# First self attention of a two-layer perceiver: projections moved ahead of the mix on TensorE, with ScalarE's copies in the same order

## The chip, the cores and the metric

One core of one Trainium2 chip runs the whole program. The metric is the device time of one execution in microseconds, the median of several. The kernel before takes 2668.17 us (median of 3, from 2666.99 to 2670.02).

## What is computed

Six stages work on a residual `x` of 64 sequences of 32 tokens with 256 features, which is 2048 rows. The change touches the code of the self attention, which is used twice, and alters the order in its first use only, the second of the six stages:

```
x = x + cross_attention_0(ctx, layernorm(x))
x = x + self_attention_0(layernorm(x))          # this stage
x = x + mixture_of_experts(layernorm(x))
x = x + cross_attention_1(layernorm(x), ctx)
x = x + self_attention_1(layernorm(x))          # rotary, through a latent
x = x + tanh_map(layernorm(x))

def self_attention_0(x):                        # 16 heads of 16 features
    q, k, v = x @ Wq.T, x @ Wk.T, x @ Wv.T      # by head
    q, k = rms_norm(q, qn_w), rms_norm(k, kn_w)
    attn = softmax(q @ k.T / 4)                 # 32 x 32 in each sequence and head
    return (attn @ v, heads side by side) @ Wo.T
```

## The kernel before, in words

The residual lies in SBUF as 16 tiles of 128 rows, so a tile holds 4 sequences. `self_attention` (line 1970) writes the code of each engine as one function `step(n, has)`, which `steps` calls for n from -6 to 16. `has(i)` says whether tile n+i exists. There is no scheduler: each engine goes through its own list in the order written, and semaphores tie the lists together. In one step the engines work on tiles of different age.

TensorE (`step` at the end of the function) does in step n:

- `scores(n+1)`: 64 products of 32x32 (L2317) into columns 0 to 127 of banks 4 to 7. It waits until the queries and keys of its tile are copied, and, by `past(pe, s.yT, n - 1)`, until the mix of the tile two before it has been copied out of the same banks.
- `queries_keys_T(n+2)`: 8 transposes (L2293) into banks 2 and 3.
- `rows_T(n+5)`: 2 transposes of the normalised rows (L2252) into bank 0.
- `output(n-1)`: 2 products (L2341) into the lower half of bank 1.
- `mix(n)`: 64 products of 32x32 (L2331), probabilities by values, into columns 128 to 191 of banks 4 to 7. It waits for the transposed probabilities and for `s.shift` of tile n+1, which says that VectorE has read the scores out.
- `values(n+4)` (2 products of 256 columns) and `project(n+4)` (2 products of 512 columns, queries and keys side by side), both at L2259. `project` writes bank 2, and so waits for the copies of queries and keys of tile n+2 out of banks 2 and 3.

A float32 product appears in the trace as two matmuls, each with a weight load of its own, and a transpose as one. So `scores` and `mix` are 128 matmuls and 128 weight loads each.

ScalarE does in step n: `queries_T(n+2)` (L2196), `exps(n+1)` (L2215), `keys_T(n+2)` (L2202), `rows_T(n+5)` (L2159), `mix_T(n)` (L2221, the copy `yT`), `values(n+4)` (two copies, L2186), `inner(n+4)` (squares, L2173, and the raw copy, L2175). VectorE does the softmax of tile n+1, adds the output of tile n-1 to the residual and takes its statistics, then rows, `queries_keys(n+3)` (L2058) and `key_sums(n+4)` (L2032). GpSimd turns those sums into inverse roots (L119, L122).

The same function, with `rotary` true, is the second self attention. Its order has one more product and larger projections.

Of the kernel before, what the change touches and what calls it, by code (L numbers as in the profile page):

```python
# [1813 lines left out]
class PlainWeights:  # L1814

    rotary = False
# [19 lines left out]
class RotaryWeights:  # L1836

    rotary = True
# [131 lines left out]
def self_attention(kit, stage, weights, norm, ahead, extra, after):  # L1970
# [4 lines left out]
    rotary, wm = weights.rotary, weights.m  # L1975
# [6 lines left out]
    with kit.stage() as st:  # L1982
# [23 lines left out]
        def past(engine, sem, value):  # L2006

            if value > 0:
                engine.wait_ge(sem, value)
# [6 lines left out]
        with nc.Block(no_gpsimd_drain=True) as block:  # L2016
# [136 lines left out]
            @block.scalar  # L2153
            def _(act):
                def rows_T(n):
                    act.wait_ge(s.xlT_ps, n + 1)

                    past(act, s.qk_ps, (n - 1) * (2 if rotary else 1))
                    nc.scalar.copy(m.xlT[:, n % 2].rearrange("p f t -> p (f t)"), kit.psum(0)[:, 0:D]).then_inc(s.xlT, 1)  # L2159

                def inner(n):
                    if rotary:

                        past(act, s.turned, n * 2)
                        for i in range(2):
                            act.wait_ge(s.qk_ps, n * 2 + i + 1)
                            if i == 1:
                                act.wait_ge(s.cosed, n * 2 + 1)
                            nc.scalar.copy(r.lat[:, i * H:(i + 1) * H, :], kit.psum(2 + i).rearrange("p (h l) -> p h l", h=H)).then_inc(s.lat, 1)
                    else:  # L2170
                        act.wait_ge(s.qk_ps, n + 1)
                        past(act, s.ss, n)
                        nc.scalar.activation(r.sq[:], kit.psum(2), ACT.Square).then_inc(s.sq, 1)  # L2173
                        past(act, s.qk, n - 1)
                        nc.scalar.copy(r.raw[:, n % 2], kit.psum(2)).then_inc(s.raw, 1)  # L2175

                def values(n):
                    act.wait_ge(s.v_ps, n + 1)
                    if n == 0:
                        act.wait_ge(s.zero, n_zero)  # L2180

                    past(act, s.y_ps, n - VB + 1)
                    src = kit.psum(1)[:, D:2 * D].rearrange("p (a i e) -> p a i e", i=2, e=EV)
                    dst = m.v[:, n % VB].rearrange("p (a i) l -> p a i l", i=2)
                    for i in range(2):
                        nc.scalar.copy(dst[:, :, i, i * EV:(i + 1) * EV], src[:, :, i, :]).then_inc(s.v, 1)  # L2186

                def queries_T(n):
                    act.wait_ge(s.qT_ps, n + 1)
                    if rotary:  # L2190
                        past(act, s.qrT_ps, n)
                        nc.scalar.copy(r.qrT[:], kit.psum(2)).then_inc(s.qrT, 1)
                    else:
                        act.wait_ge(s.gain, 1)
                        past(act, s.s_ps, n - 1)
                        nc.scalar.activation(m.qT[:, n % 2].rearrange("p c t -> p (c t)"), kit.psum(2), ACT.Identity, scale=r.gain[:]).then_inc(s.qT, 1)  # L2196

                def keys_T(n):
                    act.wait_ge(s.kT_ps, n + 1)

                    past(act, s.s_ps, n - 1)
                    nc.scalar.copy(m.kT[:, n % 2].rearrange("p c t -> p (c t)"), kit.psum(3)).then_inc(s.kT, 1)  # L2202

                def latent_T(n):
                    act.wait_ge(s.qrT_ps, n + 1)
                    if n == 0:
                        act.wait_ge(s.qb, 1)
                    past(act, s.s_ps, n - 1)
                    nc.scalar.activation(m.qT[:, n % 2].rearrange("p c t -> p (c t)"), kit.psum(2), ACT.Identity, bias=r.qb[:], scale=LS).then_inc(s.qT, 1)

                def exps(n):
                    act.wait_ge(s.shift, n + 1)

                    past(act, s.pT, n)
                    nc.scalar.activation(m.prob[:].rearrange("p h k -> p (h k)"), m.score[:].rearrange("p h k -> p (h k)"), ACT.Exp).then_inc(s.p, 1)  # L2215

                def mix_T(n):
                    act.wait_ge(s.y_ps, n + 1)

                    past(act, s.o_ps, n)  # L2220
                    nc.scalar.copy(m.yT[:].rearrange("p f (b q) -> p b f q", b=BT), mixed).then_inc(s.yT, 1)  # L2221

                def step(n, has):
                    if has(2):
                        queries_T(n + 2)
                    if has(1):
                        exps(n + 1)
                    if has(2):
                        keys_T(n + 2)
                    if has(5):  # L2230
                        rows_T(n + 5)
                    if has(0):
                        mix_T(n)
                    if rotary and has(2):
                        latent_T(n + 2)
                    if has(4):
                        values(n + 4)
                        inner(n + 4)
                    if extra is not None and n == -4:
                        extra.first_copy(act)  # L2240
                    if extra is not None and n == -3:
                        extra.second_copy(act)

                steps(step)

            @block.tensor
            def _(pe):
# [52 lines left out]
                def scores(n):  # L2300
                    if n == 0 and extra is not None:

                        pe.wait_ge(extra.w, 1)
                    pe.wait_ge(s.qT, n + 1)
                    pe.wait_ge(s.kT, n + 1)

                    past(pe, s.yT, n - 1)
                    if rotary:
                        if n == 0:
                            pe.wait_ge(s.masked, 1)  # L2310
                        for a in range(BT):
                            nc.tensor.matmul(kit.all[:, 4 + a, 0:P], kit.ident16[:], r.causal[:].rearrange("p c k -> p (c k)"), start=True, stop=False, skip_group_check=True)
                    for c in range(HC):
                        for b in range(BT):
                            for a in range(BT):
                                rows, tokens = slice(a * S, (a + 1) * S), slice(b * S, (b + 1) * S)
                                mm = nc.tensor.matmul(score[tokens, a, c, :], m.qT[rows, n % 2, c, tokens], m.kT[rows, n % 2, c, tokens],  # L2317
                                                      start=not rotary, stop=True, skip_group_check=True)
                    mm.then_inc(s.s_ps, 1)

                def mix(n, more):
                    pe.wait_ge(s.pT, n + 1)

                    if more:
                        pe.wait_ge(s.shift, n + 2)
                    for f in range(FC):
                        for i in range(2):
                            for a in range(BT):
                                for b in range(BT):
                                    rows, part, h = slice(b * S, (b + 1) * S), slice(a * S, (a + 1) * S), f * 2 * BT + 2 * a + i  # L2330
                                    mm = nc.tensor.matmul(mixed[part, b, f, :], m.v[rows, n % VB, h, :], m.pT[rows, n % 2, place(h), :],  # L2331
                                                          start=(i == 0), stop=(i == 1), skip_group_check=True)
                    mm.then_inc(s.y_ps, 1)
# [10 lines left out]
                def step(n, has):  # L2344
                    if has(1):
                        scores(n + 1)
                    if has(2):
                        queries_keys_T(n + 2, has(3))
                    if has(5):
                        rows_T(n + 5)  # L2350
                    if has(-1):
                        output(n - 1)
                    if has(0):
                        mix(n, has(1))
                    if rotary and has(2):
                        latent_T(n + 2)
                    if has(4):
                        values(n + 4)
                        project(n + 4)

                    if extra is not None and n == -4:
                        extra.first_product(pe)
                    if extra is not None and n == -3:
                        extra.second_product(pe)
# [756 lines left out]
```

## Time and profile before

| | before |
|---|---|
| median of the runs | 2668.17 us (3 runs, 2666.99 to 2670.02) |
| profiled execution, its own time | 2681.12 us |
| span of its trace | 2679.3 us |
| busy in the span | TensorE 91%, VectorE 64%, GpSimd 55%, ScalarE 48% |
| mean granted TensorE clock | 0.965 of full |
| first self attention, first transpose to last matmul | 1279.9 to 1447.9 us of the span |

The span is cut in the page into 40 slices of 67 us, so this stage is a little more than the 20th and 21st. Shares of the whole span say little about it. It is read from the timeline of its engines, window by window. A row of the timeline merges equal instructions that follow each other: start, length, engine, line, names, shape and count, and in square brackets the idle time of that engine just before them with what ended it. "issue" there is time in which the engine waited for nothing that the profile shows.

### The profile page before, as it was taken

The page shows a single profiled execution, that of the slowest core. Times are in us where ns is not written, and L with a number is a line of the kernel's source. Part 1 is how long each engine was busy: PE and PEld are TensorE (multiplying, and loading weights), DVE is VectorE, ACT ScalarE, POOL GpSimd, SP SyncE. Part 2 cuts the span into 40 slices and gives each one's busy share as a digit, 9 for nine tenths or more (in the row PEclk, how much of TensorE's full clock was granted, in tenths as well). Part 3 has the DMA queues.
Part 4 walks back from the last instruction along what each step waited for, and adds up shares of the span by engine and source line. Part 5 has one row for each costly group of instructions (what it writes and reads, how often), then busy time and mean ns, then how long its engine had stood idle before and what let it go on. Part 6 is the DMA issues. An engine that isn't in the chain of part 4 may idle for free. (4 is left out here: it accounts for less than half of the span.)

```text
span 2679.3 us, 64293 instructions
## 1 busy us (share of the span) xinstructions
PE 2450.1 (91%) x24481; PEld 1903.1 (71%) x24481; DVE 1704.3 (64%) x3966; ACT 1279.7 (48%) x2969; POOL 1469.7 (55%) x1670
## 2 busy tenths in 40 slices
PE   5887999999999999998797989489999999998997
PEld 2445887788788878786465578368888888886665
DVE  5666868687878786774475833366566665653665
ACT  2454656565656565654342323144454445443443
POOL 5776767575757576754672245555456446322333
PEclk9999999999999999998897999699999999999998
DMA  4233121111112111210003359532334234210001
GB/s 149 110 119 98 41 54 49 35 44 39 46 33 49 39 43 36 49 27 12 29 5 107 124 164 286 160 121 78 84 95 98 71 69 105 61 52 14 3 4 34
DMA packets 223075, 190.04 MB, mean 71 GB/s; under 512 B 88705, under 2 KB 210514, under 8 KB 222770
## 3 DMA queue, kind: packets, MB, share of 16 engines
q1 hardware_dynamic: 206386, 151.19, 18.8%
q0 software_dynamic: 10080, 30.00, 4.6%
q10 hardware_dynamic: 6304, 4.72, 0.6%
q8 instruction: 198, 3.24, 0.5%
q14 instruction: 107, 0.88, 0.1%
HBM read 151.53 MB, written 34.31 MB: 69 GB/s over the span
## 5 line engine op out<-in xcount | busy, mean ns | idle before, releaser
L288 POOL TENSOR_TENSOR rk<-ss,neg_half 128x32 f32<-128x32 f32 x64 | 348.7, 5448 | 246.8 <-DVE ss L270 246.8
L1695 PE MATMUL banks<-rowsT,qk 128*128 128x257 f32 x1024 | 243.3, 380 | 0.8 <-ACT qk L1622 0.8
L321 ACT ACTIVATE ksq<-kT 128x512 f32<-128x512 f32 x256 | 161.6, 631 | 160.7 <-DVE kT L264 160.5
L264 DVE COPY kT<-banks 128x512 f32<-128x512 f32 x256 | 177.0, 692 | 61.4 <-PE banks L375 56.8
L375 PE MATMUL banks<-x_hi,wk_hi 128*128 128x256 f32 x1024 | 213.1, 289 | 1.0 <-DVE kT L264 1.0
L1695 PEld LDWEIGHTS banks<-rowsT,qk 128*128 128x128 f32 x1024 | 189.5, 190 | 27.6 <-ACT qk L1622 1.2
L375 PE MATMUL banks<-x_hi,wk_lo 128*128 128x256 f32 x1024 | 206.3, 284 | 0.0
L375 PE MATMUL banks<-x_lo,wk_hi 128*128 128x256 f32 x1024 | 205.2, 281 | 0.5 <-DVE x_lo L256 0.5
L1172 ACT ACTIVATE score<-score,ntop 128x289 f32<-128x289 f32 x256 | 135.9, 533 | 118.3 <-DVE ntop L1055 118.3
L1543 POOL CAST r_hi<-diff 128x512 fp32r<-128x512 f32 x64 | 42.5, 664 | 259.5 <-PE banks L1721 256.9
L1516 POOL DMA_INDIRECT parts<-scratch_expert,address x128 | 132.0, 1031 | 92.4 <-DVE residual L1414 45.8
L375 PEld LDWEIGHTS banks<-x_hi,wk_hi 128*128 128x128 f32 x1024 | 159.1, 189 | 3.5 <-issue 3.0
L375 PEld LDWEIGHTS banks<-x_lo,wk_hi 128*128 128x128 f32 x1024 | 159.7, 190 | 0.8 <-DVE x_lo L256 0.7
L375 PEld LDWEIGHTS banks<-x_hi,wk_lo 128*128 128x128 f32 x1024 | 158.1, 188 | 0.0
L1603 ACT ACTIVATE prob<-banks,ntop 128x257 f32<-128x257 f32 x256 | 120.3, 479 | 70.1 <-DVE ntop L1430 66.9
L1430 DVE TENSOR_REDUCE ntop<-banks 128x2 f32<-128x514 f32 x128 | 88.6, 692 | 99.9 <-PE banks L1695 99.9
L1052 DVE CUSTOM_DVE_ANT_0 score<-banks,rkb 128x289 f32<-128x289 f32 x256 | 107.9, 457 | 66.0 <-PE banks L1239 57.9
L1611 ACT CAST p_hi<-banks 128x512 fp32r<-128x512 f32 x128 | 68.8, 589 | 162.6 <-PE banks L1704 153.6
L2259 PE MATMUL banks<-w,xlT 128*128 128x512 f32 (+1 forms) x320 | 133.3, 550 | 1.1 <-ACT kT L2202 0.9
L1186 ACT COPY mix<-banks 128x512 f32<-128x512 f32 x128 | 75.1, 587 | 112.1 <-PE banks L1265 112.1
L1721 PE MATMUL banks<-p_hi,r_hi 128*128 128x512 f32 x256 | 112.5, 439 | 4.3 <-ACT p_hi L1611 4.3
L1443 DVE TENSOR_TENSOR p_lo<-banks,p_hi 128x512 fp32r<-128x512 f32 x128 | 82.4, 686 | 51.3 <-ACT p_hi L1611 50.6
(369 smaller groups left out, 6544.1 us busy)
## 6 DMA issues: line engine op xcount, KB each, us to landing
rowsT<-in_ctxT SPq DMA_DIRECT2D x64, 257.0 KB
wgu<-in_expert_gu SPq DMA_DIRECT2D x64, 256.0 KB
rows<-in_ctx SPq DMA_DIRECT2D x64, 256.0 KB
raw<-in_ctx SPq DMA_DIRECT2D x61, 256.0 KB
scratch_qT<-qT SPq DMA_DIRECT2D x16, 512.0 KB, 2.6
scratch_kT<-kT SPq DMA_DIRECT2D x16, 512.0 KB, 3.0
q<-scratch_qT SPq DMA_DIRECT2D x64, 128.0 KB
kT<-scratch_kT SPq DMA_DIRECT2D x64, 128.0 KB
```

The lines of the kernel that those rows point to most:

```text
L264: nc.vector.tensor_copy(m.kT[:, k, 2 * i:2 * i + 2, 0:ROWS], banks[i % 2].rearrange("p (a r) -> p a r", a=2)).then_inc(s.kT, 1)
L288: nc.gpsimd.tensor_tensor(m.rk[:], m.ss[:], kit.neg_half[:, 0:KF * H], ALU.pow).then_inc(s.rk, 1)
L321: nc.scalar.activation(m.ksq[:, 2 * i:2 * i + 2, :], m.kT[:, k, 2 * i:2 * i + 2, 0:ROWS], ACT.Square).then_inc(s.ksq, 1)
L375: mm = nc.tensor.matmul(banks[i % 2][:, a * ROWS:(a + 1) * ROWS], w[:, f, pr * P:(pr + 1) * P], x[:, k, f, :], start=(at == 0), stop=(at = ...
L1052: nc.vector.tensor_tensor_reduce(m.score[:, c, :], score[c][:, 0:NK], m.rkb[:, c, :], 1.0, -3.0e38, ALU.mult, ALU.max, m.top[:, c:c + 1]). ...
L1172: nc.scalar.activation(m.score[:, c, :], m.score[:, c, :], ACT.Exp, bias=m.ntop[:, c:c + 1], accum_out=m.mass[:, c:c + 1]).then_inc(s.p, 1)
L1430: nc.vector.tensor_reduce(m.ntop[:, n % 2, h * HALF:(h + 1) * HALF], score[h][:, :, 0:CTX], AX.X, ALU.max, negate=True).then_inc(s.ntop, 1)
L1516: nc.gpsimd.indirect_dma_start(m.parts[:, t % 2, c, :], None, d.expert_rows, bass.IndirectOffsetOnAxis(kept.address[:, t, c:c + 1], 0)).th ...
L1603: nc.scalar.activation(m.prob[:, k, c, :], score[h][:, c - h * HALF, 0:CTX], ACT.Exp, bias=m.ntop[:, k, c:c + 1], accum_out=m.mass[:, k, c ...
L1695: mm = nc.tensor.matmul(score[h][:, c - h * HALF, 0:CTX], m.qk[:, f, j, c * BT:(c + 1) * BT, :].rearrange("p h q -> p (h q)"), m.rowsT[:, ...
L1721: mm = nc.tensor.matmul(kit.bank[3][:, f, :], lhsT, rhs, start=(at == 0), stop=(at == len(terms) - 1))
L2259: mm = nc.tensor.matmul(out, m.xlT[:, n % 2, f, :], w[:, f, columns], start=(f == 0 and not rotary), stop=(f == FC - 1))
```

## The change

For the first self attention (`rotary` false) TensorE's step ends with `project(n+4)`, `values(n+4)`, `mix(n)` in place of `mix(n)`, `values(n+4)`, `project(n+4)`. ScalarE copies the keys before it takes the exponentials, and does `inner(n+4)`, `values(n+4)`, `mix_T(n)` in place of `mix_T(n)`, `values(n+4)`, `inner(n+4)`. In both self attentions `scores` has one wait more, `past(pe, s.shift, n)`. No arithmetic changes.

```diff
@@ ScalarE
                         queries_T(n + 2)
-                    if has(1):
+                    if rotary and has(1):
                         exps(n + 1)
                     if has(2):
                         keys_T(n + 2)
+                    if not rotary and has(1):
+                        exps(n + 1)
                     if has(5):
                         rows_T(n + 5)
-                    if has(0):
-                        mix_T(n)
-                    if rotary and has(2):
-                        latent_T(n + 2)
-                    if has(4):
-                        values(n + 4)
-                        inner(n + 4)
+                    if rotary:
...
+                    else:
+
+                        if has(4):
+                            inner(n + 4)
+                            values(n + 4)
+                        if has(0):
+                            mix_T(n)
@@ TensorE, scores
                     pe.wait_ge(s.kT, n + 1)
 
+                    past(pe, s.shift, n)
                     past(pe, s.yT, n - 1)
@@ TensorE, step
-                    if has(0):
-                        mix(n, has(1))
-                    if rotary and has(2):
-                        latent_T(n + 2)
-                    if has(4):
-                        values(n + 4)
-                        project(n + 4)
+                    if rotary:
...
+                    else:
+
+                        if has(4):
+                            project(n + 4)
+                            values(n + 4)
+                        if has(0):
+                            mix(n, has(1))
```

In the middle of the stage, TensorE's list is this before (each row `x64` is one `scores` or one `mix`):

```order
L2317 MATMUL banks<-kT,qT 32x32 x64
L2293 MATMUL banks<-ident,qk 128x128 x8
L2252 MATMUL banks<-ident,xl 128x128 x2
L2341 MATMUL banks<-wo,yT 128x256 x2
L2331 MATMUL banks<-pT,v 32x32 x64
L2259 MATMUL banks<-w,xlT 128x256 x2
L2259 MATMUL banks<-w,xlT 128x512 x2
L2317 MATMUL banks<-kT,qT 32x32 x64
```

and this in the changed kernel, whose lines are numbered some ten higher:

```order
L2328 MATMUL banks<-kT,qT 32x32 x64
L2303 MATMUL banks<-ident,qk 128x128 x8
L2262 MATMUL banks<-ident,xl 128x128 x2
L2352 MATMUL banks<-wo,yT 128x256 x2
L2269 MATMUL banks<-w,xlT 128x512 x2
L2269 MATMUL banks<-w,xlT 128x256 x2
L2342 MATMUL banks<-pT,v 32x32 x64
L2328 MATMUL banks<-kT,qT 32x32 x64
```

The two projections now stand between the output and the mix, and nothing stands any more between a mix and the next scores.

ScalarE's list in one step of the same place, before:

```order
L2196 ACTIVATE qT<-banks,gain 128x512
L2215 ACTIVATE prob<-score 128x512
L2202 COPY kT<-banks 128x512
L2159 COPY xlT<-banks 128x256
L2221 COPY yT<-banks 128x4x2x32
L2186 COPY v<-banks 128x8x16 x2
L2173 ACTIVATE sq<-banks 128x512
L2175 COPY raw<-banks 128x512
```

and in the changed kernel:

```order
L2196 ACTIVATE qT<-banks,gain 128x512
L2202 COPY kT<-banks 128x512
L2215 ACTIVATE prob<-score 128x512
L2159 COPY xlT<-banks 128x256
L2173 ACTIVATE sq<-banks 128x512
L2175 COPY raw<-banks 128x512
L2186 COPY v<-banks 128x8x16 x2
L2221 COPY yT<-banks 128x4x2x32
```

The copy of the keys is one place earlier, and the copy `yT` of the mix, for which the next scores wait, is last.

## Rows read from the trace of the kernel before

**Rows 1.** The page: span, and the granted TensorE clock in 40 slices.

```profile
span 2679.3 us, 64293 instructions
...
PEclk9999999999999999998897999699999999999998
```

**Rows 2.** Timeline of TensorE (PE), one step of the stage, scores to scores.

```profile
1346.00 1.29 PE L2317 MATMUL banks<-kT,qT 32*32 32x32 f32 x128
1347.33 1.06 PE L2293 MATMUL banks<-ident,qk 128*128 128x128 f32 x8
...
1348.44 1.03 PE L2341 MATMUL banks<-wo,yT 128*128 128x256 f32 x4
1349.40 1.31 PE L2331 MATMUL banks<-pT,v 32*32 32x32 f32 x128
1350.64 2.85 PE L2259 MATMUL banks<-w,xlT 128*128 128x256 f32 x8
1353.42 0.34 PE L2317 MATMUL banks<-kT,qT 32*32 32x32 f32 x32
```

**Rows 3.** Timeline of ScalarE (ACT), the same step.

```profile
1349.37 0.57 ACT L2202 COPY kT<-banks 128x512 f32<-128x512 f32 x1
...
1350.76 0.37 ACT L2221 COPY yT<-banks 128x256 f32<-128x256 f32 x1 [0.54 <-PE banks L2331]
```

**Rows 4.** Timeline of VectorE (DVE) and GpSimd (POOL), the same step.

```profile
1346.80 0.68 DVE L2032 TENSOR_REDUCE ss<-sq 128x32 f32<-128x512 f32 x1
...
1347.87 5.43 POOL L122 TENSOR_TENSOR rss<-rss,neg_half 128x32 f32<-128x32 f32 x1
...
1349.51 0.42 DVE L2086 TENSOR_TENSOR residual<-residual,banks 128x256 f32<-128x256 f32 x1 [0.71 <-PE banks L2341]
...
1350.95 0.68 DVE L2072 TENSOR_REDUCE mass<-prob 128x16 f32<-128x512 f32 x1
...
1353.60 0.69 DVE L2058 TENSOR_TENSOR qk<-raw,rss 128x512 f32<-128x512 f32 x1
```

**Rows 5.** Windows: twelve steps; then two at half clock (TensorE alone).

```profile
1307.71:1416.38 108.67, 96.11 (x3332) 67.69 (x3331) 74.71 (x152) 47.09 (x107) 73.89 (x33) 0.94 0.02 4
...
1324.10:1327.40 3.30, 3.30 (x5) 0.50 0.03 5
...
1412.80:1416.10 3.30, 3.30 (x6) 0.50 0.02 5
```

**Rows 6.** Waits of TensorE in those twelve steps: total us, times, longest.

```profile
PE banks L2331 <- issue: 9.1, 5, 2.2
PE banks L2341 <- issue: 1.5, 3, 0.7
PE banks L2293 <- DVE qk L2058: 0.8, 1, 0.8
PE banks L2331 <- DVE score L2067: 0.7, 1, 0.7
```

**Rows 7.** Timeline of TensorE around a mix that stops halfway.

```profile
1367.67 0.25 PE L2331 MATMUL banks<-pT,v 32*32 32x32 f32 x5 [1.27 <-issue]
...
1374.19 1.02 PE L2331 MATMUL banks<-pT,v 32*32 32x32 f32 x97
1377.39 0.35 PE L2331 MATMUL banks<-pT,v 32*32 32x32 f32 x31 [2.17 <-issue]
1377.67 4.54 PE L2259 MATMUL banks<-w,xlT 128*128 128x256 f32 x8
```

**Rows 8.** Timeline of TensorE, last steps: no projections are left there.

```profile
1420.99 0.34 PE L2331 MATMUL banks<-pT,v 32*32 32x32 f32 x28 [0.38 <-issue]
1422.00 1.04 PE L2317 MATMUL banks<-kT,qT 32*32 32x32 f32 x100 [0.66 <-ACT yT L2221]
1425.34 0.34 PE L2317 MATMUL banks<-kT,qT 32*32 32x32 f32 x28 [2.30 <-issue]
```

**Rows 9.** DMA queue of one engine's instructions from 1301 to 1446 us.

```profile
q8 instruction: 35, 0.57, 1.6%
```

**Rows 10.** Windows of TensorE's matmuls (first) and weight loads (second), same stretch.

```profile
1301.00:1446.00 145.00, 121.35 (x4407) 0.90 0.02 4
...
1301.00:1446.00 145.00, 86.56 (x4405) 0.90 0.02 4
```

More of the change, by code:

```diff
@@ L2229, in step @@
                         keys_T(n + 2)
+                    if not rotary and has(1):
+                        exps(n + 1)
                     if has(5):
                         rows_T(n + 5)
-                    if has(0):
-                        mix_T(n)
-                    if rotary and has(2):
-                        latent_T(n + 2)
-                    if has(4):
-                        values(n + 4)
-                        inner(n + 4)
+                    if rotary:
+                        if has(0):
+                            mix_T(n)
+                        if has(2):
+                            latent_T(n + 2)
+                        if has(4):
[3 more added lines that the diff above has]
+                        if has(4):
+                            inner(n + 4)
+                            values(n + 4)
+                        if has(0):
+                            mix_T(n)
                     if extra is not None and n == -4:
@@ L2352, in step @@
                         output(n - 1)
-                    if has(0):
-                        mix(n, has(1))
-                    if rotary and has(2):
-                        latent_T(n + 2)
-                    if has(4):
-                        values(n + 4)
-                        project(n + 4)
+                    if rotary:
+                        if has(0):
+                            mix(n, has(1))
+                        if has(2):
+                            latent_T(n + 2)
+                        if has(4):
+                            values(n + 4)
+                            project(n + 4)
+                    else:
+                        if has(4):
+                            project(n + 4)
+                            values(n + 4)
+                        if has(0):
+                            mix(n, has(1))
                     if extra is not None and n == -4:
```

## The prediction

> **What bounds the kernel now.** I read the page first [rows 1]: 2679.3 us of span, 2.4 us under the execution's own 2681.12, and a clock row that dips in the slices of this stage. The page is an average over six stages, so I went to the timeline of the first self attention. In an undisturbed step TensorE goes from one scores to the next in 1353.42 - 1346.00 = 7.42 us, and its pieces follow each other without a gap worth the name [rows 2]: scores from 1346.00, transposes, output, mix from 1349.40, projections from 1350.64. TensorE itself is the bound. The nearest rival for it is the loop over GpSimd: sums at 1346.80, a root of 5.43 us, `qk` at 1353.60 [rows 4]. With its hand-offs this loop needs about 7.2 us, so no step can fall much under that, and the most that an unblocked loop could give is 0.2 us a step.
>
> Most steps are not undisturbed. From scores(1) to scores(13) there are twelve, and they take 108.67 us [rows 5], 19.6 more than 12 x 7.42 = 89.0. Two things fill these 19.6 us. First, TensorE stands idle 9.1 + 1.5 + 0.8 + 0.7 = 12.1 us [rows 6], 9.1 of it in the middle of mixes, for no releaser that the profile shows ("issue"). Second, four stretches of 3.4 us run at half clock, 1.2 GHz, of which the first and last stand in [rows 5]. The projections inside take 4.54 us [rows 7] in place of 2.85 [rows 2], 1.69 more each time, 6.8 us in all. Together that is 18.9 of the 19.6.
>
> **What the stops are.** Count the instructions between the two stops of [rows 7], at 1367.67 and 1377.39: 5 matmuls of mix, 8 of projections, 128 of scores, 8 and 2 transposes, 4 of output, 97 of mix make 252, with as many weight loads 504, and with the eight bare waits of a step 512, twice 256. Over the stage there are 4407 matmuls and 4405 loads [rows 10], with some 120 waits about 8930, and the instruction queue moved 35 packets of 16 KB [rows 9]: one for each 255. So TensorE's instructions come in blocks of 256, and the stops are at block ends: the next block has not arrived. In the undisturbed step a block lasts 256/564 x 7.42 = 3.4 us and nothing stops. The block that a 32x32 burst (256 instructions in 1.25 us) eats quickly is the one that comes late.
>
> The Trainium skill says otherwise in "Runtime: NRT & Kernel Launch", section "Instruction fetch mechanics": the sequencer fetches the next 16 KiB block (256 instructions) by itself, and crossing a boundary is mostly hidden, since instructions issue more slowly than blocks arrive. The block size agrees with the trace; the hiding does not, with 2.17 us of stop at one boundary. If no stop were left, the sum below would be 7.8 - 19.6 = -11.8 us, and this is the second rival.
>
> **What the change does, step by step.** No instruction is taken away; 28 bare waits are added, 14 in each self attention, on a value that an earlier wait has already seen. I price them at nothing: they stand where TensorE waits anyway or is issue-bound, and the rows of the trace put no busy time on such waits. They do move the block ends in all later stages. The second self attention is the only one with 32x32 bursts; its stops could shift by 2 us either way.
>
> Projections before mix: `project` now waits for the copy of the keys, 1349.37 + 0.57 = 1349.94 before [rows 3], while the output ends at 1349.47 [rows 2]. Because the keys' copy changes places with the exponentials, it ends about 0.6 us earlier, 1349.3, and the wait is covered. With the old order on ScalarE it would have been 0.5 us a step. The exponentials come 0.4 us later; the sum that reads them starts at 1350.95 [rows 4], over 1 us after they end, so nothing follows. `values` needs the addition of tile n-1, which ends at 1349.93 [rows 4] and has the 1.9 us of `project` as cover. The squares start 2 us earlier; the GpSimd loop takes at most 0.2 us a step from that, and TensorE, the bound, takes nothing. Mix no longer meets the wait for `shift`: 0.7 us once [rows 6].
>
> **Term 1, the copy of the mix.** Before, the 2.85 us of projections hid the copy `yT`. Now scores(n+2) stands right behind mix(n) and waits for it. The price is in the stage's last steps, where no projections are left and the order is already the new one: scores sits idle 0.66 us for `yT` [rows 8]. The copy alone is 0.37 us [rows 3]. So 0.4 to 0.7; I take 0.65, the row for the same wait. 12 x 0.65 = 7.8 us.
>
> **Term 2, instruction blocks.** Mix and scores are now 512 instructions in 1.25 + 0.65 + 1.29 us. Two block ends always fall in it, 256 instructions apart, hence 1.9 us apart, and a block needs longer. The same place in the last steps shows it: the block that begins at 1420.99 ends at 1425.34, 4.35 us, with 2.30 us of stop in the middle of scores [rows 8]. On the other side, 3.4 us a block runs unhindered [rows 2], so a block that can be asked for at once costs at most 3.4 - 1.9 = 1.5. I expect 1.4 where the boundary falls early in the mix, and 2.3 where it falls so late that the sequencer must first get past the `yT` wait; a third of the steps are of the second kind, mean 1.75. 12 x 1.75 = 21 us (ends: 0 and 12 x 2.4 = 29). The stops in the middle of mixes go: the mix now follows 4.9 us of slow instructions.
>
> **Term 3, clock.** Before, the clock fell to 1.2 GHz behind the stop of 2.17 us and not behind that of 1.27 [rows 7]. The changed step has 0.65 + 1.4 to 2.3 us idle inside 4.5 to 5.5 us of nothing but small matmuls, and what follows is slow at half clock. I take six of twelve steps, 6 x 1.69 = 10.1 us (ends: 0 and 20.3).
>
> Sum: 89.0 + 7.8 + 21 + 10.1 = 127.9 us for the twelve steps in place of 108.67, **+19.3 us**. Before the first mix and after the last projection the order hardly differs. From the profiled 2681.12 this gives 2700.4; the runs shown have a median 13 us lower, and from 2668.17 it gives **2687.5**.
>
> **Rivals.**
> 1. Only the copy costs: stops and clock stay as frequent as before, merely at other places. +7.8, 2676.0. For it: the number of blocks is the same. Against: [rows 8], where each adjacent pair stops. 12%.
> 2. Faster: the stops of mixes go with the half-clock stretches behind them, and scores stops no longer than for `yT`, because the block is fetched meanwhile. 7.8 - 19.6 = -11.8, 2656.4. It decides below 19.6/12 = 1.6 us added a step. The skill's rule would give this. For it: blocks of 3.4 us never stopped. Against: 1.9 us is far below 3.4. 10%.
> 3. The worst of terms 2 and 3 at once: 2.4 us of stop in each step and half clock in each. 7.8 + 29 + 20.3 - 19.6 = +37.5, 2705.7. For it: the block of 4.35 us. 11%.
> 4. No difference: a half-hidden copy and short stops that balance what goes. The pieces moved have slack on all other engines, so this needs a coincidence. 2668. 5%.
>
> **How the numbers follow.** My forecast has 62%; its own range is 2677 (no half clock, +9.2) to 2698 (half clock always, +29.5). The range for 8 in 10 leaves out rival 2, the upper part of rival 3 and most of rival 4: 2671 to 2704. A measurement of this kernel tells 0.2%, 5.3 us, from no change. Faster by more: rival 2, 10%. Within: rival 4 and a little of rival 1, 6%. Slower by more: 84%.
>
> **What would show it.** In the trace after: an idle of about 0.65 us before scores, ended by `yT`, in all twelve steps; stops by "issue" of 1.4 to 2.4 us inside scores, once a step, and none in mixes; steps of about 9.8 us at full clock and 11.5 with half clock; no wait of `project` for `kT`. Stops left in mixes and none in scores would make term 2 wrong; a clock that stays at 1.00 through the stage, term 3; steps of 8.1 us, rival 1 or 2.

## The result, and the profile after

The changed kernel takes 2689.72 us (median of 4, 2687.74 to 2692.46), the kernel before 2667.58 (4 runs, 2664.18 to 2670.02): ratio 1.0085, 95% interval 1.0067 to 1.0102. That is 22.1 us slower, where 19.3 were forecast.

First the page of the changed kernel: its span, and the granted clock in 40 slices, beside [rows 1].

```profile
span 2685.9 us, 64321 instructions
...
PEclk9999999999999999998887999799999999999998
```

The span is only 6.6 us longer than in [rows 1], not 22. Two windows explain most of it, each read in both kernels: the stage of this change, and the stage of the experts two stages later. Columns are the stretch, its length in us, busy us and count for TensorE, weight loads, VectorE, ScalarE, GpSimd, then clock, DMA share and GB/s. Before:

```profile
1559.80:1682.10 122.30, 105.88 (x767) 95.65 (x767) 43.46 (x128) 38.05 (x128) 60.80 (x64) 0.97 0.82 256
1276.80:1445.90 169.10, 136.05 (x4445) 95.55 (x4445) 103.84 (x205) 63.28 (x144) 107.15 (x55) 0.86 0.04 14
```

After, the same two in the other order:

```profile
1276.70:1470.40 193.70, 147.50 (x4444) 110.21 (x4445) 104.03 (x205) 61.80 (x144) 105.43 (x55) 0.79 0.04 12
...
1585.60:1692.80 107.20, 101.90 (x766) 94.75 (x766) 43.32 (x128) 41.58 (x128) 60.64 (x64) 0.95 0.89 292
```

The changed stage is 24.6 us longer. The experts' stage, which the change does not touch, was 15.1 us shorter. The two GB/s figures are no cause of this: 256 x 122.3 and 292 x 107.2 are the same bytes. In the profiled execution of the kernel before TensorE waited there for VectorE's `hidT`:

```profile
PE banks L3024 <- DVE hidT L2959: 11.5, 17, 1.3
```

A later trace of the same kernel has 0.3 us of this wait, and 106.6 us for the whole stage (run `before_again` below). Why the first trace waited is not shown. So the comparison of two single spans says 6.6 us because of an accident in another stage; the changed stage says 24.6 and the runs say 22.1.

Now the twelve steps from scores(1) to scores(13), beside the first line of [rows 5], and TensorE's waits in them, beside [rows 6]:

```profile
1307.22:1439.76 132.54, 105.22 (x3332) 80.94 (x3332) 75.68 (x154) 46.47 (x110) 72.09 (x35) 0.83 0.02 4
```

```profile
PE banks L2328 <- issue: 13.9, 8, 2.8
PE banks L2328 <- ACT yT L2221: 6.3, 11, 0.6
PE banks L2303 <- issue: 1.9, 1, 1.9
PE banks L2262 <- issue: 1.5, 1, 1.5
PE banks L2352 <- issue: 1.4, 1, 1.4
PE banks L2342 <- issue: 1.0, 2, 0.6
PE banks L2269 <- ACT kT L2202: 0.8, 1, 0.8
```

They take 132.5 us in place of 108.7. L2328 is scores, L2342 the mix, L2303 and L2262 transposes, L2352 the output, L2269 the projections. The stops of mixes, 9.1 us before, are 1.0; the scores now stop, 13.9 us in eight steps, and wait 6.3 us for `yT`, which they never did in these steps before. With the mean clock at 0.83, 2 x 0.17 x 132.5 = 45 us of the twelve steps ran at half clock, against 2 x 0.06 x 108.7 = 13 before.

One step of the timeline of TensorE, beside [rows 2]:

```profile
1349.30 0.71 PE L2328 MATMUL banks<-kT,qT 32*32 32x32 f32 x61 [0.56 <-ACT yT L2221]
1351.41 0.91 PE L2328 MATMUL banks<-kT,qT 32*32 32x32 f32 x67 [1.41 <-issue]
1352.25 1.97 PE L2303 MATMUL banks<-ident,qk 128*128 128x128 f32 x8
...
1355.44 2.74 PE L2269 MATMUL banks<-w,xlT 128*128 128x512 f32 x8
1358.12 1.29 PE L2342 MATMUL banks<-pT,v 32*32 32x32 f32 x128
1359.96 0.46 PE L2328 MATMUL banks<-kT,qT 32*32 32x32 f32 x35 [0.56 <-ACT yT L2221]
1361.82 0.91 PE L2328 MATMUL banks<-kT,qT 32*32 32x32 f32 x68 [1.40 <-issue]
```

Scores waits for the copy of the mix, does 61 of its 128 matmuls, stands 1.41 us for nothing the profile can name, and goes on. (The last row is cut off by the window; that scores has 128 too.) The transposes behind it take 1.97 us in place of 1.06 [rows 2]: half clock. From one scores to the next it is 10.7 us in place of 7.42. In the next step the stop comes behind matmul 35 and not 61. That is 26 matmuls, with their loads 52 instructions, earlier, and 52 is what the 564 instructions of a step have over 512, twice 256.

### The profile page after: what moved, and what is told of

Read it like the earlier page. It is cut to its first block and busy times, and to the rows that moved or that the text cites. A ratio compares the mean times of both kernels' runs of the same rounds, so it can differ in the third digit from the quotient of the medians.

```text
span 2685.9 us, 64321 instructions
## 1 busy us (share of the span) xinstructions
PE 2457.7 (92%) x24481; PEld 1918.1 (71%) x24481; DVE 1702.9 (63%) x3966; ACT 1280.3 (48%) x2969; POOL 1465.3 (55%) x1670
## 5 line engine op out<-in xcount | busy, mean ns | idle before, releaser
L2269 PE MATMUL banks<-w,xlT 128*128 128x512 f32 (+1 forms) x320 | 128.6, 535 | 2.0 <-ACT kT L2202 2.0
```

The lines of the kernel that those rows point to most:

```text
L2269: mm = nc.tensor.matmul(out, m.xlT[:, n % 2, f, :], w[:, f, columns], start=(f == 0 and not rotary), stop=(f == FC - 1))
```

## The experiments

Theory A, the forecast's: with the projections moved away, mix and scores are 512 instructions in one piece; the next block of 256 is late, TensorE stops, and half clock follows. Theory B: only the new wait for `yT` and what hangs on it costs, 0.65 us a step or 7.8 in all; by its size alone it does not reach 22 us. The kernel before itself took 2667.6 to 2689.4 us on the chips used, so each whole time is compared with the kernel before on its own chip, and the two orders with each other only within one group of runs. "Twelve steps" is read in each trace from scores(1) to scores(13).

**`again`**: the changed kernel, unedited.

> The changed kernel once more, beside the runs below, so that they have it on the same chip. Both theories: about 22 us above the kernel before.

Measured: ratio 1.0069 (1.0050 to 1.0088), 2706.09 against 2687.68 us, 18.4 more. Twelve steps 129.5 us. On a second chip the change costs about the same, 18.4 us for 22.1.

**`dense`**: the changed kernel with work added between mix and scores.

```diff
+                def filler(n):
+                    pe.wait_ge(s.xlT, min(n + 2, NT))
+                    for f in range(2 * FC):
+                        nc.tensor.matmul(kit.psum(0)[:, D:2 * D], m.xlT[:, n % 2, f % FC, :], w[:, f % FC, 0:D], start=True, stop=True)
...
                         if has(0):
                             mix(n, has(1))
+                        if has(0) and has(4):
+                            filler(n + 4)
```

> The changed kernel with four products of 256 columns more (8 matmuls, 1.7 us at full clock) between each of the first twelve mixes and the scores behind it. Theory A (what the change costs is that 512 instructions of 32x32 products stand in one piece: their blocks come late, TensorE idles and then runs at half clock): the added work covers the wait for yT (0.6 us) and most of the wait for the block (1.4 to 1.8 us), and the clock stays up, so the twelve steps take 118 to 126 us, less than the 132.5 of the changed kernel although work was added; the whole is 6 to 15 us faster than the changed kernel. Theory B (the change costs only the wait for yT and the slower chain behind it): 1.7 - 0.6 = 1.1 us more a step, 13 us slower than the changed kernel.

Measured, on the chip of `again`: ratio 1.0044 (1.0025 to 1.0062), 2699.92 us, 6.2 us faster than the changed kernel, with products added that take 1.9 us from their start to the next scores, 23 us in twelve steps. The twelve steps as a window, and TensorE's waits in them:

```profile
1308.90:1433.50 124.60, 113.59 (x3427) 84.11 (x3426) 75.66 (x154) 45.52 (x110) 72.51 (x35) 0.99 0.02 4
```

```profile
PE banks L2333 <- issue: 7.3, 8, 1.9
PE banks L2347 <- issue: 1.6, 4, 0.6
```

No wait for `yT` is left, the stops in scores (L2333) fall from 13.1 us in `again` to 7.3, and the clock rises from 0.86 to 0.99. Adding useless work made the twelve steps 4.9 us shorter than in `again`. Theory B wanted 13 us more; it is out as the whole cause. The added products change three things at once, the wait, the stops and the clock, so `dense` does not say which of them gave how much.

**`split_p`**: TensorE does project, mix, values; ScalarE squares and raw copy, `yT`, values.

```diff
                         if has(4):
                             project(n + 4)
-                            values(n + 4)
                         if has(0):
                             mix(n, has(1))
+                        if has(4):
+                            values(n + 4)
```

> Order project, mix, values (ScalarE: squares and raw copy, yT, values). The 0.9 us of values stand between mix and scores and cover the wait for yT. Theory A: two block ends are now 2.2 us apart in place of 1.9, so a stop of about 1.2 us stays in most scores; twelve steps 109 to 118 us, the whole 3 to 12 us slower than the kernel before. Theory B (only the wait for yT costs): no wait is left, so as fast as the kernel before within 3 us.

Measured: ratio 0.9995 (0.9977 to 1.0013): no difference from the kernel before. The twelve steps, and the largest of TensorE's waits in them:

```profile
1309.50:1425.60 116.10, 96.20 (x3331) 68.76 (x3330) 75.60 (x153) 46.26 (x108) 72.61 (x34) 0.96 0.02 4
```

```profile
PE banks L2329 <- issue: 11.9, 9, 2.2
PE banks L2343 <- issue: 2.8, 4, 0.8
PE banks L2263 <- issue: 1.7, 1, 1.7
PE banks L2304 <- issue: 1.6, 1, 1.6
```

L2329 is scores, L2343 the mix. With the smaller ones there are 19.1 us of stops, as many as in the changed kernel (19.7). What has gone is the wait for `yT` and most of the half clock: 2 x 0.04 x 116.1 = 9 us in place of 45. That the twelve steps are 7.4 us longer than in [rows 5] is within theory A's range, but its forecast for the whole kernel, 3 to 12 us slower, missed: it was 1.7 us faster, and the interval leaves at most 3.5 us of cost (0.13%). Theory B's forecast for the whole was met. So this run does not decide between the two. It does show that 0.9 us of work between mix and scores removes the cost of the change within the error of the runs, though the stops stay.

**`keys_late`**: the changed kernel, exponentials ahead of the keys' copy on ScalarE.

> The changed kernel with ScalarE's exponentials ahead of the keys' copy, as before. Both theories: project waits for kT about 0.5 us in each step, behind the output. Theory A: the blocks still bind, so the twelve steps are 3 to 8 us longer than in the changed kernel. If the wait for kT was covered by something else: no difference.

Measured: ratio 1.0072 (1.0049 to 1.0094), 1.4 us above the changed kernel. Twelve steps 130.3 us against 129.5, where 3 to 8 more were expected. A miss: `project` waits for `kT` once, 0.7 us. In the step from 1361.47 the transposes run at half clock, as TensorE's timeline shows:

```profile
1364.27 1.97 PE L2301 MATMUL banks<-ident,qk 128*128 128x128 f32 x8
1366.03 0.51 PE L2260 MATMUL banks<-ident,xl 128*128 128x128 f32 x2
1366.38 1.03 PE L2350 MATMUL banks<-wo,yT 128*128 128x256 f32 x4
1367.36 2.82 PE L2267 MATMUL banks<-w,xlT 128*128 128x512 f32 x8
```

and on ScalarE's timeline of the same step:

```profile
1366.53 0.58 ACT L2202 COPY kT<-banks 128x512 f32<-128x512 f32 x1
```

The keys' copy ends at 1367.11, late as feared, but output ends only at 1367.41. The slow clock behind the stop hides what would show at full clock. The one step with the wait agrees: there the transposes behind the stop and the output run at full clock, and the output's 1.03 us end before the copy does.

```profile
1432.91 0.70 PE L2301 MATMUL banks<-ident,qk 128*128 128x128 f32 x5 [1.84 <-issue]
1433.45 1.03 PE L2350 MATMUL banks<-wo,yT 128*128 128x256 f32 x4
1435.15 2.82 PE L2267 MATMUL banks<-w,xlT 128*128 128x512 f32 x8 [0.67 <-ACT kT L2202]
```

So that part of the change neither costs nor gains here that the runs could tell.

**`b16`** and **`a16`**: the kernel before and the changed kernel with queries and keys of this stage stored as bfloat16. A product of `scores` is then one matmul and one load, not two.

```diff
-... qT=([P, 2, HC, P], F32), kT=([P, 2, HC, P], F32), ...
+... qT=([P, 2, HC, P], F32 if rotary else BF16), kT=([P, 2, HC, P], F32 if rotary else BF16), ...
```

> The kernel before with the copies of queries and keys of the first self attention stored as bfloat16, so that each of the 64 products of scores is one matmul and one load in place of two; scores are computed from rounded queries and keys. A step has 436 TensorE instructions in place of 564. Theory A: blocks last 4.3 us, most stops in mixes go and the half clock with them: twelve steps 88 to 97 us in place of 108.7, the whole 10 to 20 us faster than the kernel before. If stops have nothing to do with instructions: only 0.6 us a step of scores go, 7 us at most.

> The changed kernel with the same bfloat16 copies. Mix and scores are together 384 instructions, so in about half of the steps only one block ends in them. Theory A: stops in half of the steps, twelve steps 97 to 110 us in place of 132.5; the gap between the two orders shrinks from 22 us to 4 to 13. Theory B (only the wait for yT): the gap stays what it was, since the wait is the same.

Measured, on one chip: `b16` 0.9910 (0.9890 to 0.9929), 24.7 us faster than the kernel before; `a16` 0.9936 (0.9915 to 0.9957), 16.3 us faster. The gap between the orders is 8.4 us in the runs (18.4 and 22.1 at full width), 15.3 in the twelve steps (23.9 at full width). The first window is `b16`, the second `a16`:

```profile
1307.50:1399.80 92.30, 80.12 (x2570) 57.83 (x2570) 73.86 (x151) 47.09 (x107) 74.22 (x33) 1.00 0.02 4
```

```profile
1306.50:1414.10 107.60, 89.95 (x2563) 66.28 (x2562) 75.13 (x154) 45.97 (x110) 72.73 (x33) 0.90 0.01 3
```

In `b16` the stops in mixes shrink from 9.1 to 2.7 us and the clock stays at 1.00, so a halved scores is worth 16.4 us in the twelve steps, of which its own shorter run explains 12 x 0.65 = 8. TensorE is no longer alone in binding there: it waits 7.4 us in eleven steps for ScalarE's copy `raw`. In `a16` the wait for `yT` is still 6.3 us, exactly that of the full-width change, while stops are 4.4 + 3.4 us and the clock is 0.90. In the runs the gap has shrunk by more than half, as theory A forecast (4 to 13 us), and not stayed, as B's forecast had it. But 8.4 us is no more than the 7.8 of the wait alone, so it is the trace, with 15.3 us, more stops and the lower clock, that speaks against B.

**`phase_b`** and **`phase_a`**: 64 bare waits more at the start of TensorE's list, in the kernel before and in the changed one.

```diff
                 pe.wait_ge(weights.loaded, weights.count)
+                if not rotary:
+                    for _ in range(128):
+                        pe.wait_ge(weights.loaded, weights.count)
```

The built list holds two of these waits in one instruction: the trace of `phase_b` has 64 semaphore instructions for the added line.

> The kernel before with 64 bare waits more at the start of TensorE's list of the first self attention, on a semaphore that is already there. Nothing else moves. Theory A: every block end stands 64 instructions earlier in the work, so each stop is found at another place of a mix or scores, by exactly 64 instructions; the time changes by less than 5 us, either way. If stops are tied to the work and not to the count of instructions: they stay where they were.

> The changed kernel with the same 64 waits. Theory A: the stops in scores move by 64 instructions and stay, one in each step; the time is within 5 us of the changed kernel.

Measured: `phase_b` 0.9983 (0.9969 to 0.9997), 4.5 us faster; `phase_a` 1.0085 (1.0058 to 1.0111), twelve steps 136.3 us. mix(1) in the kernel before, then in `phase_b`:

```profile
1319.60 1.25 PE L2331 MATMUL banks<-pT,v 32*32 32x32 f32 x125
1322.81 0.25 PE L2331 MATMUL banks<-pT,v 32*32 32x32 f32 x3 [1.96 <-issue]
```

```profile
1328.15 0.99 PE L2331 MATMUL banks<-pT,v 32*32 32x32 f32 x93
1331.33 0.46 PE L2331 MATMUL banks<-pT,v 32*32 32x32 f32 x35 [2.19 <-issue]
```

The stop has moved by 32 matmuls, which with their loads are 64 instructions. The edit leaves the work of the mix as it was; what moved is the count of instructions ahead of it. So the stops are tied to that count, and the ends of instruction blocks are what fits it. In `phase_a` the same holds for scores: the changed kernel stops behind matmul 114, 88 and 61 of scores(3), (4) and (5), and `phase_a` behind 82, 56 and 29, each 32 fewer. Ten stops in scores take 18.7 us: another phase, about the same cost.

**`act_only`**: ScalarE's new order with TensorE's old one.

> ScalarE's new order with TensorE's old one. Both theories agree that TensorE's order has to be followed: the copy yT stands behind the squares, the raw copy and the copies of values, and these wait for the projections behind the mix, so scores(n+2) waits for them, 1.9 us a step (0.60 + 0.58 + 0.43 + 0.37 less overlap). Theory A adds that this pause lies between the projections and scores, so it gives the instruction blocks time: stops in mixes get shorter. Twelve steps 120 to 132 us, the whole 12 to 22 us slower than the kernel before.

Measured: 1.0096 (1.0061 to 1.0131), 25.9 us slower; twelve steps 141.0 us, more than forecast.

```profile
PE banks L2328 <- ACT yT L2221: 20.6, 11, 1.9
PE banks L2328 <- issue: 7.1, 3, 2.9
PE banks L2342 <- issue: 4.6, 4, 1.9
```

The forecasts, 120 to 132 us and 12 to 22 us slower, both missed. The wait for `yT` is 1.9 us a step as worked out. The stops in mixes did get shorter, 4.6 us in place of 9.1, but 7.1 us appeared in scores, and with those of transposes and output all stops are 15.9 us in place of 10.6. The clock is 0.88, which is 2 x 0.12 x 141.0 = 34 us at half clock, though no mix stands next to a scores here. So ScalarE's new order with TensorE's old one costs about as much as the whole change; TensorE's new order alone was not run.

**`all16`** and **`all16_after`**: values and normalised probabilities too are bfloat16, so the mix also has 128 instructions.

```diff
-v=([P, VB, H, S], F32) ... pT=([P, 2, H, S], F32)
+v=([P, VB, H, S], F32 if rotary else BF16) ... pT=([P, 2, H, S], F32 if rotary else BF16)
+share=([P, H, S], F32 if rotary else BF16)
-nc.vector.tensor_tensor(m.prob[:], m.prob[:], m.rmass[:]...
+nc.vector.tensor_tensor(m.share[:], m.prob[:], m.rmass[:]...
...
-nc.vector.transpose(m.pT[:, n % 2]..., m.prob[:]...
+nc.vector.transpose(m.pT[:, n % 2]..., m.share[:]...
```

> The kernel before with queries, keys, values and normalised probabilities of the first self attention stored as bfloat16, so that scores and mix are 128 instructions each in place of 256; both are computed from rounded factors. A step has 308 TensorE instructions. Theory A: no stop of over 1 us is left in the twelve steps and no half clock; TensorE is no longer the bound, the loop over GpSimd (7.2 us) is: twelve steps 86 to 92 us, the whole 22 to 32 us faster than the kernel before. If stops have nothing to do with the count of instructions: 14 us at most.

> The changed kernel with the same bfloat16 factors. Mix and scores are together 256 instructions, so one block ends in them and not two. Theory A: no stop in scores; only the wait for yT (0.6 us) is left of the change's cost, and TensorE has slack for it: within 5 us of the old order with the same factors. Theory B (the wait for yT is all the cost there is, on a TensorE that bounds): also small here, but it has to explain why the gap of 22 us at full width has gone, while the wait is the same.

Measured: `all16` 0.9895 (0.9866 to 0.9924), 29.8 us faster than the kernel before; `all16_after` 0.9868 (0.9839 to 0.9896), 34.9 us faster. The windows of the twelve steps, `all16` first, and then the waits of `all16_after`:

```profile
1308.80:1396.20 87.40, 72.60 (x1795) 50.38 (x1794) 73.77 (x151) 45.89 (x107) 73.44 (x33) 1.00 0.01 3
```

```profile
1307.30:1397.00 89.70, 75.99 (x1795) 52.49 (x1794) 74.39 (x152) 46.40 (x110) 73.53 (x33) 0.96 0.01 3
```

```profile
PE banks L2328 <- ACT yT L2221: 6.7, 11, 0.6
PE banks L2303 <- DVE qk L2058: 5.5, 10, 1.2
PE banks L2269 <- ACT kT L2202: 0.8, 1, 0.8
```

This is the cleanest reading of the stops: with half the instructions in mix and scores there are none in them, in either order. The changed order keeps its wait for `yT`, 6.7 us, all of it, and yet the 24 us between the orders in the twelve steps are 2.3. TensorE waits for `qk` instead (14.0 us in `all16`, 5.5 in `all16_after`), the loop over GpSimd, at 7.3 us a step. The same 0.6 us a step costs next to nothing once TensorE is not the bound. For that reason the vanished gap does not by itself speak against theory B; the vanished stops do speak for A. In the runs the changed order is even the faster, 2631.7 to 2636.3 us against 2638.5 to 2644.1. This is not the stage's doing, which from its first transpose to its last matmul takes 140.3 us in `all16` and 140.8 in `all16_after`; where the 5 us come from is open.

**`before_again`**: the kernel before, unedited, on the chip of the last three.

> The kernel before as a run of its own, for a trace from the same chip as the others. Ratio 1.000. Its stage takes 169 us as in the first trace, within 3 us.

Measured: ratio 1.0003 (0.9988 to 1.0019); stage 172.3 us, twelve steps 109.6, stops of mixes 10.3 us in 6. The two traces of this kernel differ by 3.2 us on the stage, a little more than the 3 expected, and by 0.9 on the twelve steps. With this trace the change costs 21.4 us in the stage (193.7 - 172.3) and not 24.6.

## Why the prediction was right, step by step

- **What bounds, and what the stops are.** Right. The counting of instructions between two stops was enough to call them block ends, and `phase_b` moved one by exactly the 64 instructions that were put in front. The rule of the Trainium skill ("Runtime: NRT & Kernel Launch", "Instruction fetch mechanics") that crossings are mostly hidden does not hold here where 256 instructions pass in 1.25 us; the measured stops decide.
- **Term 1**, forecast 7.8 us: the waits view has 6.3. Right: it is 0.57 us a time in place of 0.65. But `all16_after` shows that it is a cost only while TensorE binds.
- **Term 2**, forecast 21 us: stops are 13.9 + 1.9 + 1.5 + 1.4 + 1.0 = 19.7 us. Right in size and place, with one error of form: not "once a step" inside scores but eight times in twelve. In the other steps the stop stands among the transposes or in the output, where a later block ends, or there is none. The forecast wanted 2.3 us in a third of the steps; there are two such stops (2.5 and 2.8 us), the other six last 1.2 to 1.6.
- **Term 3**, forecast 10.1 us: the rest, 132.5 - 89.0 - 6.3 - 19.7 - 0.8 = 16.7 us, goes with 45 us at half clock. Undersized: in the timeline half clock came in nine of the twelve steps, not in six, and in some of them for twice as long: 1327.5 to 1334.1 is one stretch of 6.6 us at 0.50. From the start of the transposes to the start of the projections the nine steps have together about 12.6 us more than at full clock, stops left out, and the projections 3.2 us more, 15.8 of the 16.7. So it fell mostly on transposes and output (1.97 in place of 1.06 for the transposes) and less on the projections from whose rows it was priced. How this term divides is worked out, not measured by an experiment of its own. `dense` and `split_p` show that most of it goes when work stands between mix and scores. That the half clock follows from the stops, as this term has it, is not shown (see the last section).
- **What was left out**, 0.8 us: `project` does wait for `kT`, once, in the first of the twelve steps, where the forecast had no such wait.
- **The sum**: 127.9 us forecast for the twelve steps, 132.5 measured in the first trace and 129.5 in the second; in the runs +22.1 for +19.3. The terms were off by -1.5, -1.3, +6.6 and +0.8 us, so the closeness of the total owes a little, not much, to errors that cancel.
- **Covers.** That with the old order on ScalarE the keys' copy would cost 0.5 us a step was wrong in effect: `keys_late` lost nothing, since half clock made the cover longer. Nothing was priced for it, so the sum did not suffer.
- **Rivals.** Only the copy costs (2676): out by the measured 2689.7 itself and by `dense`. Faster: the stops did leave the mixes, 9.1 to 1.0 us, as that rival said, but more came back in scores. The worst case (2705.7) had stops of 2.4 us in each step; their mean is 1.7.
- **The later stages.** 14 waits more in the second self attention moved nothing that can be seen: from its first transpose to the end of the span are 2679.3 - 2453.2 = 226.1 us in the trace before and 2685.9 - 2460.0 = 225.9 after.

## What to carry to other kernels

When an engine idles for "issue" in a burst of tiny instructions, count instructions between such stops; a constant distance, here a multiple of 256, points to the supply of instructions, and some instructions put in front of the list test it. In this kernel it paid to keep one burst apart from the next by slow instructions that are few: 0.9 us of them (`split_p`) were enough to lose the 22 us, by covering the wait for `yT` and by keeping the clock up, while the stops stayed. Fewer instructions helped more than any order tried: halving both bursts (in bfloat16, where the result allows it) took 30 to 35 us off this kernel, and made the order that cost 22 us free. Both versions beat both kernels. They compute from rounded factors.

## What the runs showed that was not expected

- Half clock does not follow from a long stop alone. The twelve steps of `phase_b` have ten stops in mixes of together 12.7 us, up to 2.5 us long (16.4 us with those elsewhere, 10.6 in the kernel before), and a clock of 1.00 throughout, while the kernel before with 9.1 us of them in mixes has 0.94:

```profile
1314.10:1423.30 109.20, 90.90 (x3331) 66.49 (x3330) 75.54 (x152) 47.04 (x107) 73.74 (x33) 1.00 0.02 4
```

  Both take the same time, 109.2 and 108.7 us. What decides the clock here stays open; that it fell behind the stop of 2.17 us and not behind that of 1.27, from which the forecast argued, was true of one trace. `split_p` says the same of stops in scores: nine of them, up to 2.2 us long, at a clock of 0.96. So that adjacent bursts bring half clock is seen in `after`, `again` and `phase_a`, but the link from stop to half clock, on which term 3 rests, is not shown.
- Useless work can pay: `dense` runs 23 us of added products and is 6 us faster than the same order without them. It is still 12 us slower than the kernel before.
- Queries and keys in bfloat16 were expected to give `b16` 10 to 20 us and gave 24.7 (19 to 30 by the interval). The twelve steps give 16.4 of it; the whole stage, first transpose to last matmul, takes 147.5 us in its trace against 168.0 before, so the steps around the twelve gained about 4 us more.
